# A fused convolution and window-attention kernel: the first image loaded ahead of the tap weights, the tap sums and a clearing moved from VectorE to GpSimd, the halving of the taps moved into ScalarE's copies

## The reference

```
x = x + conv3x3(group_norm(x), W0)                        # 256 -> 256 channels, padding 1
x = x + batch_norm(proj(linear_attention(group_norm(x)))) # windows of 4 x 4 points
```

## Time and profile before

| | us |
|---|---|
| median of 3 runs | 2502.22 |
| lowest and highest | 2491.29, 2502.49 |
| the profiled execution's own time | 2488.01 |
| its span | 2486.1 |

### The profile page before, as it was taken

How to read it: one execution, slowest core, us unless ns; L and a number is a source line. 1 busy time by engine, 2 the same in 40 slices (tenths; PEclk the granted TensorE clock), 3 DMA queues, 4 the chain that set the end, 5 groups by cost and what they waited for, 6 DMA issues and landing times.

```text
span 2486.1 us, 112351 instructions
## 1 busy us (share of the span) xinstructions
PE 2389.9 (96%) x49576; PEld 2162.7 (87%) x49576; DVE 1970.8 (79%) x3608; ACT 1280.5 (52%) x3352; POOL 1169.2 (47%) x2364
## 2 busy tenths in 40 slices
PE   4999999999999999999999999999999999999998
PEld 4998889888898888988889888898889978898887
DVE  8887868888688886878858788687886878865886
ACT  2137751377514774157731577316772267722775
POOL 0026760277503775047740477305772067712776
PEclk9999999999999999999999999999999999999999
DMA  4000010000100002000010000100001000000000
GB/s 166 1 2 14 17 61 16 2 16 15 65 12 2 16 19 72 1 2 19 19 68 1 6 15 19 69 1 6 19 15 69 1 9 15 21 11 2 16 15 24
DMA packets 38959, 58.19 MB, mean 23 GB/s; under 512 B 4688, under 2 KB 36304, under 8 KB 36560
## 3 DMA queue, kind: packets, MB, share of 16 engines
q1 hardware_dynamic: 38736, 55.27, 6.3%
HBM read 29.57 MB, written 25.69 MB: 22 GB/s over the span
## 4 chain that ended last, share of the span: by engine, by line
PE 95%; issue 2%; DVE 1%; ACT 0%; DMA 0%; POOL 0%; SPq 0%; POOLq 0%; DVEq 0%
PE ps L334 34%; PE ps L405 15%; PE ps L353 11%; PE ps L394 10%; PE ps L380 9%; PE ps L360 9%; PE ps L369 4%; PE ps L414 3%; DMA xs<-w_conv 0%; PE ps L319 0%; DVE st L772 0%; PE ps L561 0%; PE ps L345 0%; ACT ve L613 0%; DVE xh L914 0%
## 5 line engine op out<-in xcount | busy, mean ns | idle before, releaser
L334 PE MATMUL ps<-dp,wc 128*128 128x392 f32 x4608 | 844.7, 343 | 5.6 <-issue 5.6
L334 PEld LDWEIGHTS ps<-dp,wc 128*128 128x128 f32 x4608 | 821.0, 189 | 11.3 <-issue 9.7
L1138 POOL TENSOR_TENSOR ve<-vpraw,vmask 128x1024 f32<-128x1024 f32 x200 | 392.1, 1961 | 364.6 <-ACT vpraw L624 364.6
L405 PEld LDWEIGHTS ps<-at,wp 128*128 128x128 f32 x3200 | 376.3, 192 | 49.6 <-DVE kvm L954 46.3
L1109 POOL TENSOR_TENSOR qm<-qraw 128x64 f32<-128x64 f32 x200 | 59.5, 298 | 763.2 <-ACT qraw L631 763.2
L914 DVE TENSOR_SCALAR xh<-xs,gn 128x128 f32<-128x128 f32 (+3 forms) x560 | 407.9, 781 | 0.5 <-PE ps L360 0.2
L405 PE MATMUL ps<-at,wp 128*128 128x128 f32 (+1 forms) x3200 | 405.5, 280 | 1.0 <-ACT yb L647 1.0
L595 ACT CAST dp<-dt 128x896 fp32r<-128x896 f32 x128 | 120.9, 944 | 513.4 <-PE ps L334 423.6
L353 PE MATMUL ps<-wkv,xt 128*128 128x512 f32 x1200 | 324.6, 406 | 7.1 <-issue 7.1
L613 ACT ACTIVATE ve<-ps,vmask 128x256 f32<-128x256 f32 x800 | 314.2, 490 | 0.0
L833 DVE TENSOR_TENSOR xs<-xs,ps 128x392 f32<-128x392 f32 x384 | 201.1, 558 | 125.0 <-PE ps L334 124.2
(11 more groups left out here) (87 smaller groups left out, 2898.9 us busy)
## 6 DMA issues: line engine op xcount, KB each, us to landing
out<-xs SPq DMA_DIRECT2D x224, 112.0 KB, 1.8
xs<-x SPq DMA_DIRECT2D x16, 1344.0 KB, 9.7
xs<-x SPq DMA_DIRECT2D x16, 224.0 KB, 2.7
xs<-w_conv SPq DMA_DIRECT2D x1, 2304.0 KB, 9.0
kvm<-w_kv SPq DMA_DIRECT2D x1, 512.0 KB, 14.2
wp<-w_proj SPq DMA_DIRECT2D x4, 128.0 KB, 7.8
wq<-w_q SPq DMA_DIRECT2D x1, 256.0 KB, 14.1
gav<-gavg SPq DMA_DIRECT2D x1, 64.0 KB, 8.7
```

Of the source, the lines that this page charges most:

```text
L334: last = nc.tensor.matmul(ps[:, conv_bank(v, mt), 0:CONV_N], wc[:, part_w, k, kt * TAPS + dy, mt * P:(mt + 1) * P], dp[:, kk % 2, part_d, ...
L405: last = nc.tensor.matmul(ps[:, BANK_A + mt, Y0:Y0 + n], wp[:, q, mt * P:(mt + 1) * P], at[:, q, e, 0:n], start=(q == 0), stop=(q == QUADS ...
L1138: nc.gpsimd.tensor_tensor(ve[:, t % 2, :, 1].rearrange("p e (n m) -> p e n m", m=DIM + 1)[:, :, :, 0:DIM], vpraw[:].rearrange("p (n m) -> ...
```

## The change

Five edits, all ahead of the regular part:

1. SyncE issues the first image as two transfers (one a channel half, each with a semaphore of its own) ahead of the taps, and the taps in two halves with `gav` between them.
2. The tap sums run on GpSimd in two halves of three additions each, without the halving. Their scratch `wouter` lies in `qs` and no longer in `xp`.
3. The halving is a scale (`TAP_SCALE`) in ScalarE's copies, which are eight half copies now (`taps_high`), with the group norm's root and the first two input copies between them; and a scale in VectorE's low part (`taps_low`, now a scalar_tensor_tensor).
4. The clearing of `ve` runs on GpSimd.
5. VectorE makes the statistics of each image half as it lands, and then the group norm; `taps_low` of the first tap set and `low_parts(0)` come after the first product input and ahead of the second.

```diff
--- before.py
+++ after.py
@@ -22,6 +22,7 @@
 
 
 PRODUCTS = (1, 2, 0, 3)
+TAP_SCALE = (1.0, 0.5, 0.5, 1.0)
 PARTS = ((0, 0), (0, 1), (1, 0))
 PAIRS = W // 2
 CONV_H = 14
@@ -188,20 +189,21 @@
         ps = ctx.enter_context(nc.psum_tensor("ps", [P, 8, 512], F32))
 
 
-        xp_flat = xp[:].rearrange("p k y x -> p (k y x)")
         kvm_flat = kvm[:].rearrange("p h r c -> p (h r c)")
         wkv_raw = kvm_flat[:, 0:KT * 2 * C].rearrange("p (k o) -> p k o", k=KT)
         poolm_raw = kvm_flat[0:TT, KT * 2 * C:KT * 2 * C + TT]
         wspace = xs[:, 1].rearrange("p k n -> p (k n)")
         wraw = wspace[:, 0:TAPS * TAPS_K].rearrange("p (a x o) -> p a x o", x=TAPS, o=C)
         wsum = wspace[:, TAPS * TAPS_K:(TAPS + 1) * TAPS_K].rearrange("p (a o) -> p a o", o=C)
-        wouter = xp_flat[:, 0:TAPS_K].rearrange("p (a o) -> p a o", o=C)
+        wouter = qs[:].rearrange("p m e n -> p (m e n)")[:, 0:TAPS_K].rearrange("p (a o) -> p a o", o=C)
         wprod = (wraw[:, :, 0, :], wsum, wraw[:, :, 1, :], wraw[:, :, 2, :])
 
 
+        x_first_loaded = [sem(f"x_first_loaded{kt}") for kt in range(KT)]
         x_loaded = sem("x_loaded")
         x_tail_loaded = sem("x_tail_loaded")
         w_loaded = sem("w_loaded")
+        w_rest_loaded = sem("w_rest_loaded")
         gav_loaded = sem("gav_loaded")
         bn_loaded = sem("bn_loaded")
         c_loaded = sem("c_loaded")
@@ -286,10 +288,11 @@
                                  xs_row(b, mt, row)).then_inc(stored, DMA)
 
             sp.dma_start(bnp[:], bn).then_inc(bn_loaded, DMA)
-            sp.dma_start(wspace[:, 0:TAPS * TAPS_K], w_conv).then_inc(w_loaded, DMA)
+            for kt in range(KT):
+                sp.dma_start(xs[:, 0, kt, :], x[0, kt * P:(kt + 1) * P, :]).then_inc(x_first_loaded[kt], DMA)
+            sp.dma_start(wraw[:, 0:TAPS], w_conv[:, 0:1]).then_inc(w_loaded, DMA)
             sp.dma_start(gav[:], gavg).then_inc(gav_loaded, DMA)
-            load_x(0, 0)
-            load_x(0, 1)
+            sp.dma_start(wraw[:, TAPS:KT * TAPS], w_conv[:, 1:2]).then_inc(w_rest_loaded, DMA)
             for dst, src in ((wq[:], w_q), (wkv_raw, w_kv), (poolm_raw, pool_m), (idn[:], ident), (hm[:], hmask),
                              (vwin[:], vinit[:, NWIN, 0, 0:NWIN])):
                 sp.dma_start(dst, src).then_inc(c_loaded, DMA)
@@ -298,8 +301,6 @@
                 sp.dma_start(wp[32 * g:32 * g + 32], w_proj[:, g, :].rearrange("(q i) o -> i q o", q=QUADS)).then_inc(c_loaded, DMA)
 
             sp.wait_ge(c_loaded, CONSTS * DMA)
-            sp.wait_ge(x_loaded, KT * DMA)
-            sp.wait_ge(x_tail_loaded, KT * DMA)
             sp.wait_ge(w_ready, len(PRODUCTS))
             load_x(1, 0)
             load_x(1, 1)
@@ -588,6 +589,12 @@
                 act.wait_ge(gn_var, n + 1)
                 nc.scalar.activation(dev[:, 3, :], dev[:, 2, :], ACT.Sqrt).then_inc(root_ready, 1)
 
+            def taps_high(k, kt):
+
+                a = slice(kt * TAPS, (kt + 1) * TAPS)
+                nc.scalar.activation(wc[:, 0, k, a], wprod[k][:, a], ACT.Copy,
+                                     scale=TAP_SCALE[k]).then_inc(w_high, 1)
+
             def split(v):
                 act.wait_ge(d_ready, v + 1)
                 if v >= 2:
@@ -703,13 +710,22 @@
             nc.scalar.activation(bnt[:, 1, :], bnt[:, 0, :], ACT.Sqrt).then_inc(bn_ready, 1)
 
             act.wait_ge(w_loaded, DMA)
-            for n, k in enumerate((0, 3, 1, 2)):
-                if n >= 2:
-                    act.wait_ge(w_step, n + 2)
-                nc.scalar.copy(wc[:, 0, k], wprod[k]).then_inc(w_high, 1)
+            taps_high(0, 0)
+            taps_high(3, 0)
+            act.wait_ge(w_step, 2)
+            taps_high(1, 0)
             root(0)
-            for v in range(2):
-                split(v)
+            act.wait_ge(w_step, 3)
+            taps_high(2, 0)
+            act.wait_ge(w_rest_loaded, DMA)
+            taps_high(0, 1)
+            taps_high(3, 1)
+            act.wait_ge(w_step, 5)
+            taps_high(1, 1)
+            split(0)
+            act.wait_ge(w_step, 6)
+            taps_high(2, 1)
+            split(1)
             act.wait_ge(c_loaded, CONSTS * DMA)
             nc.scalar.copy(wkv[:, 0], wkv_raw).then_inc(att_w_high, 1)
 
@@ -860,9 +876,9 @@
                         add_product(v, 1)
                         if at in STATS_AT:
                             if STATS_AT[at] == 0:
-                                dve.wait_ge(x_loaded, (b + 2) * (KT * DMA))
+                                dve.wait_ge(x_loaded, (b + 1) * (KT * DMA))
                             if STATS_AT[at] == CHUNKS - 1:
-                                dve.wait_ge(x_tail_loaded, (b + 2) * (KT * DMA))
+                                dve.wait_ge(x_tail_loaded, (b + 1) * (KT * DMA))
                             stats_x(b + 1, STATS_AT[at])
 
             def first_chunk(b):
@@ -984,7 +1000,6 @@
                         normalize_tile(b, s + 4)
                         tile_low(b, s + 4)
 
-            nc.vector.memset(ve[:], 0.0).then_inc(set_up, 1)
             for q in range(QUADS):
                 nc.vector.memset(qmask[32 * q:32 * q + 32, q % 2:q % 2 + 1], 1.0)
                 nc.vector.memset(qmask[32 * q:32 * q + 32, 1 - q % 2:2 - q % 2], 0.0)
@@ -1016,29 +1031,16 @@
             for k in range(4):
                 nc.vector.memset(dev[:, k, :], 0.0).then_inc(conv_added, 1)
 
-            def w_do(n, ins):
-                ins.then_inc(w_step, 1)
-                dve.wait_ge(w_step, n)
-
-            g0, gsum, g1, g2 = wprod
-            dve.wait_ge(w_loaded, DMA)
-            w_do(1, nc.vector.tensor_tensor(wouter, g0, g2, ALU.add))
-            w_do(2, nc.vector.tensor_tensor(gsum, wouter, g1, ALU.add))
-            w_do(3, nc.vector.tensor_scalar(gsum, gsum, 0.5, None, ALU.mult))
-            w_do(4, nc.vector.tensor_tensor(g1, wouter, g1, ALU.subtract))
-            w_do(5, nc.vector.tensor_scalar(g1, g1, 0.5, None, ALU.mult))
-
             def taps_low(k):
-                dve.wait_ge(w_high, len(PRODUCTS))
-                nc.vector.tensor_tensor(wc[:, 1, k], wprod[k], wc[:, 0, k].bitcast(F32),
-                                        ALU.subtract).then_inc(w_ready, 1)
-
-            taps_low(PRODUCTS[0])
-            dve.wait_ge(x_loaded, KT * DMA)
-            for c in range(CHUNKS):
-                if c == CHUNKS - 1:
-                    dve.wait_ge(x_tail_loaded, KT * DMA)
-                stats_x(0, c)
+                dve.wait_ge(w_high, {1: 7, 2: 8}.get(k, 6))
+                nc.vector.scalar_tensor_tensor(wc[:, 1, k], wprod[k], TAP_SCALE[k], wc[:, 0, k].bitcast(F32),
+                                               ALU.mult, ALU.subtract).then_inc(w_ready, 1)
+
+            for kt in range(KT):
+                dve.wait_ge(x_first_loaded[kt], DMA)
+                for i in range(CHUNKS):
+                    last = nc.vector.bn_stats(st0[:, kt, i, :], xs[:, 0, kt, i * CHUNK:(i + 1) * CHUNK])
+            last.then_inc(st0_done, CHUNKS)
             dve.wait_ge(st0_done, CHUNKS)
             dve.wait_ge(conv_added, 4)
             channel_stats(0, st0)
@@ -1046,8 +1048,9 @@
             group_variances(0)
             group_norm_end(0, gn0)
             product_inputs(0)
+            taps_low(PRODUCTS[0])
+            low_parts(0)
             product_inputs(1)
-            low_parts(0)
 
             for k in PRODUCTS[1:]:
                 taps_low(k)
@@ -1151,6 +1154,20 @@
                             xrow, ALU.add)
                 last.then_inc(out_ready, 1)
 
+            def taps(kt):
+
+                a = slice(kt * TAPS, (kt + 1) * TAPS)
+                g0, gsum, g1, g2 = (w[:, a] for w in wprod)
+                pool.wait_ge(w_rest_loaded if kt else w_loaded, DMA)
+                nc.gpsimd.tensor_tensor(wouter[:, a], g0, g2, ALU.add).then_inc(w_step, 1)
+                pool.wait_ge(w_step, 3 * kt + 1)
+                nc.gpsimd.tensor_tensor(gsum, wouter[:, a], g1, ALU.add).then_inc(w_step, 1)
+                pool.wait_ge(w_step, 3 * kt + 2)
+                nc.gpsimd.tensor_tensor(g1, wouter[:, a], g1, ALU.subtract).then_inc(w_step, 1)
+
+            nc.gpsimd.memset(ve[:], 0.0).then_inc(set_up, 1)
+            for kt in range(KT):
+                taps(kt)
             for b in range(B):
                 pool_q(b, 0)
                 spread_pooled(b, 0)
```

## The result

| | kernel before | changed |
|---|---|---|
| median, us | 2497.80 (22 runs) | 2490.39 (22 runs) |
| lowest and highest | 2489.62, 2502.49 | 2480.79, 2497.62 |
| ratio, 95% interval | | 0.9976 [0.9967, 0.9985] |

The change makes the kernel 6.0 us faster (3.7 to 8.2), a quarter of a percent.

The account below looks back on a forecast made before the run. TensorE's work was 95% of the chain, but VectorE's string through `low_parts(1)` set the second product's start: -12.7 + 5.1 + 1.8 = -5.8 us, taking the 2502.2 us median to 2496, range 2483 to 2505.

Parts of the forecast that it names:

- the sum at the second product: Opening, up to the second product's start: -12.7 + 5.1 + 1.8 = -5.8 us, starting at 41.4 instead of 47.23.
- Statistics earlier: VectorE's statistics run as the image halves land, so aggregation starts at 15.95 instead of 28.65: 12.7 us earlier.
- The curve of bytes moved before: Opening transfers: earlier byte curve plus 1.4 us puts image halves at 8.2 and 12.2, taps at 15.0 and 18.0.
- Standing still: Group norm on VectorE: tiny tensor_tensors with SBUF inputs wait until GpSimd's running additions end, together 5.1 us.
- Low taps: VectorE's `taps_low(1)` moves between product input and `low_parts(0)`, adding 1.76 us to the path; bounds 1.76 and 2.7.
- An addition of GpSimd: Tap sums on GpSimd: six additions of 768 elements at 1.5 us each, at most 1.9; a skill-based estimate gave 1.7.
- The clearing: Clearing of `ve` on GpSimd: taken as 3.9 us and hidden, upper bound 8.8.
- ScalarE's copies: Eight half tap copies on ScalarE of some 0.75 us, the scale costing nothing; hidden by 2.9 us.
- Rival C: TensorE's clock falls in the larger hole before the second product, costing 1.7 us: -4.1, 2498 us; chance 0.09.
- The time of 2496: Whole kernel: 5.8 us taken from the 2502.2 median of three runs gives 2496.4, predicted as 2496.
- Rival D: Opening's gain eaten: scalar_tensor_tensor at 2.7, additions 1.9, clearing 8.8, up to 3.8 + 2 + 3; 2502 us; chance 0.07.
- wrong altogether: Sign of failure: the stretch behind the second product changes length beyond what the clock explains; no change was forecast there.

Follow-up runs that it names:

- short_sums: Changed kernel with GpSimd's tap additions cut from 256 to 8 columns a tap (output wrong); second product started at 36.09 us instead of 40.41.
- beside_adds: Kernel before plus four unread GpSimd additions of 768 elements, started with the group norm's first step; second product at 51.09 us instead of 47.23.
- changed_again: Changed kernel unaltered, timed a second time beside the kernel before; median 2492.21 us (12 runs), ratio 0.9988 [0.9970, 1.0005].
- clear_on_dve: Changed kernel with the clearing of `ve` back on VectorE; second product started at 40.00 us instead of 40.41.
- beside_memsets: Kernel before plus four unread GpSimd memsets of 2048 elements, started with the group norm's first step; second product at 47.43 us instead of 47.23.
- taps_first: Changed kernel with both tap halves and the group sums' matrix transferred ahead of the image again; second product at 41.38 us instead of 40.41.

## Why the prediction was right

The forecast was 5.8 us less time, and 6.0 (3.7 to 8.2) was measured, 3.0 in the second timing; the sum at the second product was -5.8, and the trace shows -6.8. The path and its terms were right. That 6.0 comes so near 5.8 is partly luck, since neither the stretch of low clock behind the hole nor the lower mean clock was in the sum. Its three terms:

- **Statistics earlier, -12.7:** 12.66. Image half 0 landed at 8.4 (8.2 forecast), the taps at 15.0 (15.0). The curve of bytes moved before with 1.4 us on top was good to 0.2 us, since nothing but the order changed.
- **Standing still, +5.1:** 4.3. L768 1.04, L770 1.50, L781 0.23, L783 1.51 above their 0.16 or 0.17. The mechanism is right and shown from both sides (short_sums, beside_adds); the list of the instructions that are held was not. I had every small tensor_tensor wait for an addition of its own. Two of them (L769, L782) slip into the 0.1 us between two additions, because the one before them was released by the end of an addition. And I had left out the tensor_scalar, although the row that I argued from, L914, is a tensor_scalar. So two waits of 1.5 us fell away and one of 1.5 came in, and that the sizes agree is partly luck. (The 5.1 is also not quite what the prediction's own times give: with P6 done at 24.6 the group norm is done at 25.0 and not 25.3, which makes it 4.8.)
- **Low taps, +1.8:** 1.6: from the end of the group norm to the second product it is 15.9 us now and was 14.3. (L1036 takes 1.75 as scalar_tensor_tensor, like the tensor_tensor of the earlier trace rows.)

An addition of GpSimd takes 1.81 us, not the 1.5 that I scaled from its rows, one of which has an input that is broadcast; my upper bound of 1.9 held, and the estimate of 1.7 from GPSIMD Engine Reference in the Trainium skill was nearer. It hardly mattered: 0.3 us on each addition moved the ends that VectorE waits for, but the pairs that slipped through made up for it. The clearing took 3.94 against 3.9. ScalarE's copies, 0.84 with a scale instead of the 0.75 that I had, stayed hidden: VectorE's low tap ran at 27.87 without a wait.

Rival C, the clock falling in the larger hole, was set as an alternative with a chance of 0.09. It was no alternative but came on top, 1.25 us of the 6.8, and so the profiled opening is worth 5.6. It isn't there in every execution: in changed_again the clock fell 0.9 us after the first product had started, and that product took 8.20 us instead of 6.64; the hole shrank to 1.49 and the second product started at 40.46 at full clock. There VectorE's string hid the loss, as the prediction said of the first product.

The time of 2496 was 5.6 above the measured median, 4.4 of it the level from which it was counted: the first three runs of before had a median of 2502.2, all 22 have 2497.8. Rival D's sum was off too: 3.8 + 2 + 3 less 5.8 is 3 us slower, 2505 and not 2502. It didn't come: scalar_tensor_tensor took 1.75 us, an addition 1.81, the clearing 3.94.

I had written that I would be wrong altogether if the stretch behind the second product changed by more than the clock explains. It is 2486.1 - 47.23 = 2438.9 us before and 2493.0 - 40.41 = 2452.6 after, 13.7 longer. Summed over the trace's granted clock, this stretch falls 15.3 us short of full clock before and 23.1 after, so the clock explains 7.8 of the 13.7. By the letter that sign of being wrong came true for this pair of executions, and where the other 6.0 come from stays open. They are not clearly the change's, though. With the lost clock taken off, the stretch is 2423.5 us in before and 2429.5 in after; in beside_adds and beside_memsets, the kernel before with a few more instructions on GpSimd, it is 2429.9 and 2433.1, and in short_sums and clear_on_dve, built on the changed kernel, 2425.0 and 2428.2. So it differs by several us between executions of kernels that have this stretch in common, and a sign of 6 us can't be read from one pair. How often the clock falls is another matter: over many executions the changed kernel's mean clock was lower than the other's (0.9912 and 0.9931, table above), which a prediction that ends at the second product leaves out.

## What to carry to other kernels

Work moved to GpSimd is not free for VectorE: while an addition runs there, VectorE's next instruction with two SBUF inputs stands still to the end of it, however small it is, and a tensor_scalar from SBUF to SBUF can too (L783 did, the filling of `xp` did not). So put such work beside VectorE instructions with one input (statistics, here), never beside a chain of small dependent steps, where every step can pay a whole addition. And when an edit moves one engine's string, ask at once where the hole in the bound engine ends: here `low_parts(1)` ahead of the set-up work was worth 4.0 us against one profiled execution of the changed kernel and 2.8 against the other, about half of what the whole change brought.

## What the hardware showed

- A GpSimd memset of 3.94 us held a tensor_scalar of two elements for 2.1 us; four memsets of 1.8 us held no tensor_tensor, and one of them a tensor_scalar of two elements for 0.3 us. VectorE's statistics, aggregation, reciprocals and the filling of `xp` (2.06 us for both halves) kept their lengths beside the additions.
- TensorE's clock fell to the lower level within the hole of 3.05 us in the changed kernel and in short_sums, and 1.2 us behind it in taps_first. Behind the hole of 2.03 of the kernel before it stayed full, but in beside_memsets, with 2.06, it fell 1.5 us behind it: the length of the hole alone doesn't decide. A matmul of 392 columns takes 528 ns from start to end at the lower level and 340 at the full one, but matmuls overlap, so this isn't the price: in changed_again 3.4 us at the lower level made the first product 1.56 us longer (8.20 against 6.64), a little under half of the stretch.
